# A graph, attention and expert block on one core: stored blocks with 128 rows, and raw products copied two batches later

## What is computed

```
xn = layernorm(x)
norm = w * rsqrt(deg_out[src] * deg_in[dst] + eps)
h6 = relu(segment_sum((xn @ W6)[src] * norm, dst) + b6)
h7 = relu(segment_sum((h6 @ W7)[src] * norm, dst) + b7)
gnn = h7 @ Wp + bp
q, k, v = four heads of xn @ wq.T, xn @ wk.T, xn @ wv.T ; layernorm of k and v per head
mix = (q @ (k.T @ v / N)) heads joined @ wo.T + bo
x = x + gnn + mix
x = x + layernorm(experts(layernorm(x)) + layernorm(x))     # top 2 of 8 experts, the same two for every row
```

## Time and profile before

| | us |
|---|---|
| median of 3 runs | 3768.61 (3756.12 to 3771.73) |
| the profiled execution's own time | 3737.88 |
| its span | 3736.1 |
| PE busy | 2989.6 (80%) |
| POOL busy | 2160.5 (58%) |
| DVE busy | 1794.4 (48%) |
| ACT busy | 1148.4 (31%) |
| queue q0 (gathers), share of 16 engines | 23.0% |
| queue q1 (SyncE's transfers), share of 16 engines | 20.2% |

### The profile page before, as it was taken

How to read it: one execution, slowest core, us unless ns; L and a number is a source line. 1 busy time by engine, 2 the same in 40 slices (tenths; PEclk the granted TensorE clock), 3 DMA queues, 4 the chain that set the end, 5 groups by cost and what they waited for, 6 DMA issues and landing times.

```text
span 3736.1 us, 52490 instructions
## 1 busy us (share of the span) xinstructions
PE 2989.6 (80%) x16152; PEld 2000.4 (54%) x16152; DVE 1794.4 (48%) x4526; ACT 1148.4 (31%) x4063; POOL 2160.5 (58%) x2090
## 2 busy tenths in 40 slices
PE   5777737888887888888874588788897888888998
PEld 4444514565555555555552356465565555655666
DVE  9888735666666666656541221422311244222334
ACT  5787734444443443434320100100100111002211
POOL 5666546676766666666765666566665666630000
PEclk8999967999999999999986799899898889998999
DMA  4331134454444544445455455455555554543221
GB/s 124 99 98 51 50 71 133 140 167 140 155 158 143 162 143 160 151 138 162 129 158 159 129 157 187 121 186 176 154 190 181 171 160 148 177 146 108 77 77 47
DMA packets 238808, 511.75 MB, mean 137 GB/s; under 512 B 61281, under 2 KB 128647, under 8 KB 232935
## 3 DMA queue, kind: packets, MB, share of 16 engines
q0 software_dynamic: 88704, 243.35, 23.0%
q1 hardware_dynamic: 143317, 258.49, 20.2%
q10 hardware_dynamic: 6500, 6.40, 0.5%
HBM read 382.96 MB, written 125.15 MB: 136 GB/s over the span
## 4 chain that ended last, share of the span: by engine, by line
PE 49%; another core or an unknown queue 11%; issue 7%; DVE 6%; ACT 3%; DMA 3%; SPq 3%; DVEq 1%; ACTq 1%; POOL 1%; POOLq 0%
PE ps L688 21%; PE ps L666 9%; PE ps L857 5%; PE ps L870 4%; PE ps L649 4%; DMA ab<-in_x 3%; SPq L2019 2%; ACT ab L1720 1%; PE ps L628 1%; PE ps L805 1%; PE ps L808 1%; DVE ab L1285 1%; DVE mlb L1252 1%; ACT mlb L1734 1%
## 5 line engine op out<-in xcount | busy, mean ns | idle before, releaser
L1943 POOL DMA_INDIRECT ringb<-t,src x1848 | 1852.9, 1003 | 982.6 <-issue 498.2
L688 PE MATMUL ps<-xb,ab 125*128 125x256 f32 (+1 forms) x4700 | 1215.0, 402 | 87.1 <-issue 72.6
L688 PEld LDWEIGHTS ps<-xb,ab 125*128 125x128 f32 x4700 | 927.1, 201 | 343.1 <-issue 181.1
L666 PE MATMUL ps<-mlb 128*125 128x300 f32 x1260 | 477.0, 471 | 171.9 <-ACT side L1724 75.6
L1720 ACT ACTIVATE ab<-ps 125x250 f32 x724 | 294.2, 406 | 730.0 <-remote 319.2
L649 PE MATMUL ps<-ringb,Sb 128*32 128x257 f32 (+1 forms) x3696 | 341.2, 421 | 134.3 <-issue 58.7
L666 PEld LDWEIGHTS ps<-mlb 128*125 128x125 f32 x1260 | 227.7, 204 | 332.5 <-issue 298.4
L1916 POOL TENSOR_TENSOR ab<-ab,wn 128x100 f32<-128x100 f32 x201 | 272.6, 1360 | 180.3 <-DVE ab L1068 180.3
L590 PE MATMUL ps<-ab 128*50 128x125 f32 x3228 | 228.3, 286 | 143.3 <-issue 55.7
L1252 DVE TENSOR_TENSOR mlb<-iof,rel 128x900 f32<-128x900 f32 (+1 forms) x231 | 232.5, 1007 | 162.0 <-remote 101.5
L590 PEld LDWEIGHTS ps<-ab 128*50 128x50 f32 x3228 | 182.3, 131 | 212.9 <-issue 122.9
(11 more groups left out here) (228 smaller groups left out, 2702.2 us busy)
## 6 DMA issues: line engine op xcount, KB each, us to landing
ad<-ab SPq DMA_DIRECT2D x42, 1562.5 KB
ab<-ad SPq DMA_DIRECT2D x210, 312.5 KB
ringb<-t,src POOLq DMA_INDIRECT x1848
kvd<-mlb SPq DMA_DIRECT2D x50, 250.0 KB
kvb<-kvd SPq DMA_DIRECT2D x50, 250.0 KB
x2t<-mlb SPq DMA_DIRECT2D x13, 500.0 KB
xb<-x2t SPq DMA_DIRECT2D x13, 500.0 KB, 8.4
xb<-in_x SPq DMA_DIRECT2D x10, 625.0 KB
```

The costliest lines, as they stand in the source:

```text
L666: e.matmul(PS[bank_of(t)][0:R, 0:HR], low[:, slot_of(t), :], high[:, slot_of(t), :], start=True, stop=True).then_inc(s_bld, 1)
L688: ins = e.matmul(PS[3][:, 0:wd], lhs, X[0:R, k, 0:wd], start=k == 0, stop=k == NT - 1)
L1943: e.indirect_dma_start(msg[:, slot * QT + k, 0:width], None, table, bass.IndirectOffsetOnAxis(src[:, t:t + 1], 0)).then_inc(s_g[slot], 16)
```

## The change

The DRAM tensors ad (adjacency blocks) and kvd (raw keys and values) get 128 rows instead of 125, and every store to them and load from them covers all 128 partitions. The three added rows are never used in a product; to give them a value, VectorE clears partitions 96 to 127 of the part of ab behind the one-hots of the front, and of raw, ahead of its first batch (semaphore s_pad, waited for by ScalarE's first raw copy). In the front the raw product of tile i goes to bank PS[5] or PS[6] by the parity of i, TensorE waits for the raw copy i-2 rather than i-1, and ScalarE's copy comes five batches after the transposition instead of three. All other transfers keep their 125 rows.

```diff
-assert KV_AT[-1] + 4 < len(BATCHES)
+assert KV_AT[-1] + 5 < len(BATCHES)
...
-        kvd = dram("kvd", [N, 2 * D])
+        kvd = dram("kvd", [NT, P, 2 * D])
...
-        ad = dram("ad", [DY, R, AP_])
+        ad = dram("ad", [DY, P, AP_])
...
+        s_pad = sem("s_pad")
...
             def kv_product(i):
...
-                if i >= 1:
-                    e.wait_ge(s_krc, i)
+                if i >= 2:
+                    e.wait_ge(s_krc, i - 1)
                 for h in range(2):
-                    ins = e.matmul(PS[5][0:R, :], xT[:, i % 2, h, :], wkv[:, h, :], start=h == 0, stop=h == 1)
+                    ins = e.matmul(PS[5 + i % 2][0:R, :], xT[:, i % 2, h, :], wkv[:, h, :], start=h == 0, stop=h == 1)
...
             e.memset(dsum, 0.0).then_inc(s_dcp, 1)
+            e.memset(ab[P - W:P, HOT:2 * AP_], 0.0).then_inc(s_pad, 1)
+            e.memset(raw[P - W:P, :, :], 0.0).then_inc(s_pad, 1)
...
             def kv_raw(i):
                 k = i % 2
                 e.wait_ge(s_kmm, i + 1)
+                if i == 0:
+                    e.wait_ge(s_pad, 2)
                 if i >= 2:
                     e.wait_ge(l_kr[k], 16 * loads_of(i - 1, k))
-                e.activation(raw[0:R, k, :], PS[5][0:R, :], ACT.Copy).then_inc(s_krc, 1)
+                e.activation(raw[0:R, k, :], PS[5 + k][0:R, :], ACT.Copy).then_inc(s_krc, 1)
...
-                if c - 3 in KV_AT:
-                    kv_raw(KV_AT.index(c - 3))
+                if c - 5 in KV_AT:
+                    kv_raw(KV_AT.index(c - 5))
...
-                e.dma_start(kvd[i * R:(i + 1) * R, :], raw[0:R, k, :]).then_inc(l_kr[k], 16)
+                e.dma_start(kvd[i], raw[:, k, :]).then_inc(l_kr[k], 16)
...
-                e.dma_start(kin[0:R, k, :], kvd[i * R:(i + 1) * R, :]).then_inc(l_kx[k], 16)
+                e.dma_start(kin[:, k, :], kvd[i]).then_inc(l_kx[k], 16)
...
-                e.dma_start(ad[d][:, p * SW:(p + 1) * SW], ab[0:R, o:o + SW]).then_inc(l_as[d % 2], 16)
+                e.dma_start(ad[d][:, p * SW:(p + 1) * SW], ab[:, o:o + SW]).then_inc(l_as[d % 2], 16)
...
-                    e.dma_start(ab[0:R, q * PW:(q + 1) * PW], ad[d][:, q * PW:(q + 1) * PW]).then_inc(l_ap[p], 16)
+                    e.dma_start(ab[:, q * PW:(q + 1) * PW], ad[d][:, q * PW:(q + 1) * PW]).then_inc(l_ap[p], 16)
```

## The result

The changed kernel takes 3733.05 us (median of 4 runs, 3721.43 to 3736.57) where the kernel before takes 3770.01 us beside it: ratio 0.9899, 95% interval 0.9877 to 0.9921, that is 37 us faster. The forecast was 3689 us, 80 us faster, in a range of 3630 to 3745. The profiled execution took 3731.11 us, its span 3729.3. In the changed kernel the lines shift by 1 to 5: TensorE's 688 is 689, 649 is 650, VectorE's 1437 is 1440, SyncE's 2019 is 2024. In runs with other edits they shift likewise, so a row is told by its tiles.

What follows compares the result with a forecast made beforehand. VectorE was taken to bound the early front, TensorE to be busiest in the layers, 125-row transfers saturating five DMA engines in layer 2. Front -27, layer 2 -46, turn -7 made -80: 3689 us, range 3630 to 3745.

Steps and rivals of the forecast that it cites:

- The front edits: Late front: VectorE regains 26 us of waiting for TensorE; between 130 and 250 us, 5 us of waiting for ScalarE.
- Layer 2, forecast -46: Layer 2 with 128-row loads: 25 us Sb wait, 5 before line 688, 5 before line 698, 11 of clock.
- 58.9 us of "issue" before line 688: Layer 2, TensorE's unexplained idle: 5 us saved, taken as late parts of A; ends 0 and 20.
- 11 us of clock: Layer 2: a tenth of about 108 us lost to TensorE's lower clock after idles is won; ends 0 and 40.
- 214 us: Layer 2: GpSimd's idle before gathers beyond mere issue, read as ring-slot waiting; the most the gathers allow as gain.
- rival (a): Layer 2 gains more, as building and chunk turns also waited for blocked queues: 100 + 15 + 27, 3627 us; chance 0.18.
- The x load: Layer 2 epilogue's 125-row in_x load queues behind block loads; VectorE waits 110.4 us, delaying Sb for TensorE.
- Rival (c): Only the front gains; the x load's 25 us are its own or SyncE's order, or 128 rows don't widen: 3742, chance 0.09.
- The turn, forecast -7: Entry to layer 2: A's last stores and loads leave the engines of the first gathers sooner, 7 us saved.
- The clearing, forecast +4: Start of front: VectorE's two memsets stand exposed ahead of the first batch, costing 4.1 us.
- SyncE's order, set at 0: Front: stores waiting longer for the raw copy delay x loads, against freed DMA engines; 0 us, ends -3 and +10.
- rival (e): Slower: wide block transfers crowd gathers on all engines and TensorE stands, 3868 us; chance 0.05.

Runs made afterwards that it cites:

- split_120_3: Kernel before, each adjacency block transfer sent as 120 and 5 rows, nothing cleared; repeated when gathers had no stops: 0.9577, 148 us faster.
- split_120: Kernel before, each adjacency block store and load sent as 120 and 5 rows, nothing padded or cleared: 0.9946, 20 us faster.
- store128_load125: Kernel before with adjacency blocks stored with 128 rows and padding of ab cleared, but loaded back with 125: 1.0001.
- before_again: Kernel before, unchanged, run for a second profile in the picture with gather stops: 0.9989.
- after_again: Changed kernel, unchanged, run for a second profile in the picture with gather stops: 0.9879 against the kernel before.
- before_3: Kernel before, unchanged, profiled again when gathers had no stops: 1.0003, the kernel before taking 3519.84 us beside it.
- after_3: Changed kernel, unchanged, profiled again when gathers had no stops: 0.9548 against the kernel before, 159 us faster.
- before_idle: Kernel before with GpSimd made to stand still some 1.2 us before every eighth gather: 1.0408 against the kernel before, 3666.07 us.
- after_idle: Changed kernel with GpSimd made to stand still some 1.2 us before every eighth gather: 1.031 against the kernel before, 3629.75 us.
- front_only: Kernel before with only the front edits: raw copy two batches later, two banks, no 128 rows or clearing: 0.9963, 14 us faster.
- blocks_only: Kernel before with only adjacency blocks stored and loaded with 128 rows and ab's padding cleared: 0.9923, 29 us faster.
- x_on_act: Kernel before with layer 2's in_x load and result store issued on ScalarE's queue instead of SyncE's, blocks still 125 rows: 0.9979.
- x_on_act_3: Kernel before with layer 2's in_x load and result store on ScalarE's queue, repeated when gathers had no stops: 1.0001.
- kvd_only: Kernel before with only raw keys and values stored and loaded with 128 rows and raw's padding cleared: 1.0004.
- front_rows_later: Kernel before with front_only's edits, plus transposed-row copy and product one batch later and SyncE's stores two batches later in its order: 0.9936.
- pool_clear: Changed kernel with the two padding clearings on GpSimd instead of VectorE: 0.9555 against the kernel before, 160 us faster.
- best2: Changed kernel with front_rows_later's edits, clearings on GpSimd, and layer 2's in_x load and result store on ScalarE's queue: 0.9532 against the kernel before.

## Why the prediction was right and wrong

**Direction and mechanism.** Right. 125-row transfers run on a third of the engines and are the cause: the earlier trace rows repeated in the profile after, and split_120_3 gets 148 of 159 us with 120 rows and no padding. By the rule of the Trainium skill's page "DMA: Bandwidth & Descriptors", section "Why a DMA increments its semaphore by 16 and not by 1", 120 rows go to 15 engines and 125 to 5; this case agrees, with 5.4 engines busy at 125 rows and the gain of split_120; that it is 15 for 120 rows no row here shows by itself. The loads and not the stores are what counts (store128_load125).

**Where the time went.** The span of a profiled execution falls into five stretches: the front up to the first gather, layer 1 to its last chunk lift, the turn to the first chunk lift of layer 2, layer 2 to its last, and the rest. After minus before, in us, rounded:

| pair | front | layer 1 | turn | layer 2 | rest | span |
|---|---|---|---|---|---|---|
| forecast | -27 | 0 | -7 | -46 | 0 | -80 |
| before, after | -14 | +9 | -5 | +3 | 0 | -7 |
| before_again, after_again | -13 | 0 | +1 | -30 | 0 | -43 |
| before_3, after_3 (no stops) | -14 | 0 | -14 | -129 | 0 | -157 |
| before_idle, after_idle | -13 | -2 | -2 | -19 | +3 | -32 |

The medians of the first two pairs differ by 37 and 41 us.

**The step that failed** is the size of two terms. The front edits were put at 26 + 5 = 31 us, and front_only gave 14. The wide loads were put at 46 + 7 = 53 us, and blocks_only gave 29, or some 33 with its clearing of 4.4 us taken out. The 17 and 20 us between are nearly all that the forecast had too much. In both terms waits that go were counted as time won, with a wrong answer (the front) or none (layer 2) to what the engines would wait for next. What that was follows under Front and Layer 2.

**Layer 2, forecast -46.** Measured -30 in the second pair of profiles (1209 to 1179), -35 in blocks_only (to 1175), +3 in the first pair. Term by term: the 25.4 us of TensorE waiting for Sb went whole, as said. The 5 us taken from the 58.9 us of "issue" before line 688 failed: it grew to 64.8, and from 44.8 to 58.8 us in the second pair, while before_3 has 4.8. This idle time belongs to the picture with stops and not to the blocks; the prediction had called it late parts of A. The 5 of the 10.7 us before line 698 came in both pairs (4.4 and 4.3 are left), though blocks_only still has 15.8. The 11 us of clock did not come whole: the granted clock was 0.91 in both first profiles, 0.91 against 0.92 in the second pair, where TensorE's busy time fell by 6 us (1011 to 1005); in the first it rose by 7.

What took the rest can be seen at GpSimd. Its idle time ahead of the first gather of each step splits into the part before the product that frees the ring slot had ended, in which TensorE really holds it, and the part after, the stops. By that split TensorE holds GpSimd for 74 and 98 us in layer 2 of before and before_again, and for 68, 38 and 32 us in after, after_again and blocks_only; the stops are 141 and 122 us before, 144, 151 and 149 after. (The ends of the products are modelled by the profile, so these are estimates.) In the second pair TensorE lets GpSimd go 60 us sooner, and 28 us of that come back as longer stops, which leaves about the 30 us that were measured. So the prediction's 214 us "in which it waits for ring slots", its upper end, were at most 98 us of waiting for TensorE. Its own row gave 91.1 us to TensorE and had 122.5 us without a name, which should have been kept apart.

A rule comes out of the runs without the chip's own stops: the stage is as long as the slower of two streams. The gathers of layer 2 need 1009 us (after_3), about 1135 with stops by hand; the narrow loads with TensorE behind them need 1146 to 1154. Removing the second bound wins 130 us against the first pace and 19 against the second. With the chip's own stops the rule alone does not give the number: GpSimd's gathers, issue and unnamed waits add up to 1098 us in after_again, whose layer 2 takes 1179. For rival (a), a larger gain in layer 2, a chip without stops is the case, and there it is larger than its 100 + 15 us: 130 + 13.

**The x load.** The prediction made in_x the victim through which the blocks cost time, and so did I in x_on_act's expectation. The victim was named rightly (110.4 to 7.4 us) but it was not the cause's only way: shorten its wait and TensorE waits for the blocks instead, 120.6 us in all where it was 120.4 (x_on_act_3). Rival (c), that the wait is SyncE's order, is out.

**The turn, forecast -7.** 136 us in both traces before, 131 and 137 in two after; 133 to 119 without the stops. Its ends were 0 and 15.

**Layer 1, forecast 0.** Right: 1481 and 1481 us in the second pair, 1315 and 1315 without the stops; in the first pair 1482 and 1491, inside its ends. Without stops GpSimd never stands still for 1.2 us behind the first gather, in either kernel, so the gathers set the pace there, and the wider stores had nothing to shorten (store128_load125 1.0001, kvd_only 1.0004).

**Front, forecast -27.** Measured -13 to -14. The raw copy's wait went whole, as forecast. "Who is next?" was answered with an engine, VectorE, from busy times; next was an instruction of the same engine, the copy of the transposed rows, which reads a product of the batch just before exactly as the raw copy had done. VectorE got back 11 of its 28 us, and a late batch takes 2.03 us where the prediction's sign was 1.9. front_rows_later moved that too and brought the front to -24.5 us (504.9 to 480.4), near the 26 + 5 forecast for the wait. The clearing, forecast +4 and exposed: 5.4 us at the first batch (12.1 to 17.5). At the front's end blocks_only shows 4.4 of them; beside the front edits under 1 is left (front_only 491.5, after_again 492.3), yet pool_clear's first gather is 4.7 us before after_3's. In time, pool_clear and after_3 can't be told apart (0.9555 and 0.9548). SyncE's order, set at 0 with an end of +10: VectorE waited 10.1 us for x rows in front_only and 6.7 in after, where it had waited 0.3; the prediction had named this as a sign of being wrong, and it came.

**Crowding out, rival (e).** No sign in the times: after is faster in every pair. TensorE's wait for gathers (22.0 us in after_3) comes beside gathers that follow each other without a gap, so it is that of a stream at its own pace.

**The profile's own time.** I made the sum against an execution of 3737.88 us, 0.8% under the median. In the second pair the profiled executions (3746.58 and 3703.85) differ by 43 us, as the medians do by 41; in the first pair by 7, where the medians differ by 37. The first profile of each side by itself would have said that next to nothing was gained.

## What to carry over

Before pricing the removal of one bound, write down the pace of the stream that runs beside it, with every kind of idle time of that engine under its own name. The gain ends where that stream becomes the slower one: the same edit was worth 19 us in layer 2 beside one pace and 130 beside another. In this kernel transfers of 128 rows, or of 120 and a rest, beat those of 125, on the loads that the path waits for; giving one starved load a queue of its own only moved the shortage. When a wait at one instruction is removed, look for the next instruction on the same engine that depends on the same batch.

## What was not expected of the hardware

In some executions GpSimd stops for 1.2 to 3 us ahead of the first gather of a step although the ring slot is free by the trace, and in others never, the same chip included. The start times of the gathers behind a stop fit a grid of about 6.0 us in layer 1, but 6.0 us is also the mean length of a step there (1482 us for 246 steps), so the grid points at no cause by itself. With the stops layer 1 is 167 us longer (1315 to 1482), and TensorE shows idle "issue" time of 45 to 65 us in layer 2 where it is under 5 without. The two go together in part: of TensorE's 49 unexplained waits of 0.8 us or more in layer 2 of before_again, 24 overlap an unnamed stop of GpSimd, though these fill only 9% of the stage. The handmade stops bring the gain of the change down to the same size but show none of that second part; how much of the 37 to 45 us it took is open, as is the cause of the stops.

The fastest kernels here are best1, the change with the front edits of front_rows_later and the clearing on GpSimd, 0.9535 [0.9523, 0.9547], and best2 with 0.9532 [0.952, 0.9544]; they can't be told apart. The changed kernel had 0.9548 [0.9519, 0.9577] beside a kernel before of the same time, so the intervals overlap. The first gather of best1 comes 10.5 us earlier than that of after_3 (491.0 to 480.5).
